# Both Softplus halves of a state-space block in a row on ScalarE at slot 24, with a new table of slots

## The reference

```
z, x, B, C, dt_raw = split(u @ in_proj_w.T)
dt = softplus(dt_raw @ dt_proj_w.T + dt_proj_b)          # 256 channels per token
h  = exp(dt[..., None] * A) * h + (dt * x)[..., None] * B # a scan over the tokens, 32 states per channel
y  = sum over states of h * C;  y = (y + x * D) * silu(z) @ out_proj_w.T
mlp = silu(xn @ gate_w.T) * (xn @ up_w.T) @ down_w.T      # 704 hidden
```

## Time and profile before

| | us |
|---|---|
| median of 3 runs | 1143.21 (1143.1 to 1143.37) |
| the profiled execution | 1142.64 |
| its span | 1140.6 |
| PE, DVE, POOL, ACT busy | 1027.5, 1009.3, 931.2, 627.9 |
| first scan of tiles 0 to 7 starts at | 38.3, 150.3, 280.0, 407.6, 536.1, 663.6, 792.0, 919.5 |

### The profile page before, as it was taken

How to read it: one execution, slowest core, us unless ns; L and a number is a source line. 1 busy time by engine, 2 the same in 40 slices (tenths; PEclk the granted TensorE clock), 3 DMA queues, 4 the chain that set the end, 5 groups by cost and what they waited for, 6 DMA issues and landing times.

```text
span 1140.6 us, 13548 instructions
## 1 busy us (share of the span) xinstructions
PE 1027.5 (90%) x3844; PEld 537.2 (47%) x3844; DVE 1009.3 (88%) x1133; ACT 627.9 (55%) x1235; POOL 931.2 (82%) x540
## 2 busy tenths in 40 slices
PE   3566689999999999999999999999999989899998
PEld 1222134546454554546453554546453543446777
DVE  4689899999999999999999999999999989997342
ACT  4464675548655675548655675548655554443320
POOL 2689899888999899888999899888999989886100
PEclk9696689999999999999999999999999989899999
DMA  6999899998979798998989798988979797860000
GB/s 230 227 209 196 187 237 245 234 194 187 230 180 218 166 232 192 210 198 189 227 186 214 166 239 185 216 196 189 232 176 204 165 229 163 175 148 19 0 1 18
DMA packets 120121, 208.41 MB, mean 183 GB/s; under 512 B 16816, under 2 KB 25968, under 8 KB 119920
## 3 DMA queue, kind: packets, MB, share of 16 engines
q1 hardware_dynamic: 118320, 203.85, 79.8%
q0 software_dynamic: 1008, 3.67, 0.9%
q10 hardware_dynamic: 720, 0.04, 0.0%
HBM read 178.65 MB, written 12.06 MB: 167 GB/s over the span
## 4 chain that ended last, share of the span: by engine, by line
PE 59%; POOL 15%; issue 8%; ACT 8%; DVE 7%; DMA 1%; SPq 1%; DVEq 0%; POOLq 0%; ACTq 0%
PE p_r L560 17%; PE p_r L549 11%; POOL h_s L1352 9%; PE p_y L515 7%; PE p_r L555 6%; PE p_dt L504 5%; DVE h_s L1083 4%; POOL bt_s L1322 3%; PE p_r L566 2%; PE p_dt L660 2%; PE p_r L660 2%; ACT p_dt L716 2%; PE p_r L535 2%; ACT tok L765 2%; PE p_r L670 1%
## 5 line engine op out<-in xcount | busy, mean ns | idle before, releaser
L1352 POOL TENSOR_TENSOR h_s<-h_s,c_s 128x1024 f32<-128x1024 f32 x255 | 601.9, 2365 | 69.9 <-DVE h_s L1083 52.2
L716 ACT ACTIVATE p_dt<-p_dt,an_s 128x512 f32<-128x512 f32 x400 | 260.7, 660 | 274.2 <-PE p_dt L504 273.9
L1083 DVE TENSOR_TENSOR_SCAN h_s<-p_dt,carry,bt_s 128x512 f32<-128x512 f32 x256 | 319.4, 1271 | 7.8 <-ACT p_dt L716 7.2
L1083 DVE TENSOR_TENSOR_SCAN h_s<-p_dt,bt_s 128x512 f32<-128x512 f32 x256 | 303.2, 1211 | 15.5 <-ACT p_dt L716 13.3
L504 PE MATMUL p_dt<-kdt,pick_s 128*128 128x512 f32 x400 | 253.5, 647 | 56.3 <-DVE h_s L1083 44.2
L1322 POOL TENSOR_TENSOR bt_s<-bt_s,b_s 128x1024 f32<-128x1024 f32 x101 | 239.0, 2366 | 12.3 <-DMA bt_s<-dx_rows 7.5
L560 PE MATMUL p_r<-nT,w_s 128*128 128x512 f32 x448 | 208.3, 601 | 0.3
L1066 DVE TENSOR_TENSOR bt_s<-bt_s,p_b 128x1024 f32<-128x1024 f32 x155 | 186.3, 1202 | 8.8 <-DMA bt_s<-dx_rows 8.8
L504 PEld LDWEIGHTS p_dt<-kdt,pick_s 128*128 128x128 f32 x400 | 78.6, 200 | 193.8 <-DVE h_s L1083 104.1
L515 PE MATMUL p_y<-h_s,ysel_s 128*32 128x512 f32 x1024 | 143.1, 633 | 14.8 <-POOL h_s L1352 14.5
L549 PE MATMUL p_r<-nT,gu_s 128*128 128x512 f32 x308 | 144.6, 599 | 5.9 <-ACT nT L916 5.9
(11 more groups left out here) (153 smaller groups left out, 955.4 us busy)
## 6 DMA issues: line engine op xcount, KB each, us to landing
bt_s<-dx_rows SPq DMA_DIRECT2D x512, 256.0 KB, 5.7
dtr_s<-dt_rows SPq DMA_DIRECT2D x224, 128.0 KB, 6.5
kdt<-st_dt SPq DMA_DIRECT2D x64, 128.0 KB, 5.4
tok<-in_x SPq DMA_DIRECT2D x8, 512.0 KB, 8.5
xo<-in_x SPq DMA_DIRECT2D x8, 512.0 KB, 3.8
xr_s<-xb_s SPq DMA_DIRECT2D x64, 64.0 KB, 5.5
b_s<-xb_s SPq DMA_DIRECT2D x64, 64.0 KB, 5.2
dx_rows<-dx_s SPq DMA_DIRECT2D x16, 256.0 KB, 6.5
```

Source lines behind the costliest of these rows:

```text
L716: A(p_dt[DT_BANK[u]][:, :], dt_in, ACT.Exp, scale=an_s[:, c:c + 1]).then_inc(a_dA, 1)
L1083: V.tensor_tensor_scan(h_s[:, u % 8, :], p_dt[DT_BANK[u]][:, :], bt_s[:, u % 16, :], carry[:, u:u + 1] if par else 0.0, ALU.mult, ALU.add) ...
L1352: G.tensor_tensor(h_s[:, two, :], h_s[:, two, :], c_s[:, h, :].unsqueeze(1).broadcast_to([P, 2, T]), ALU.mult)\
```

## The change

The matmul of `dtp1` moves from slot 53 to slot 24, right behind that of `dtp0`. Both Softplus stand in slot 25 one after the other. The second writes to a new SBUF tile `dt1_s`, which takes the place of `dt_s` and of the PSUM bank for that half; its rounded copy, low part and `dt * x` stay in slots 55 and 57. The bank of `dtp1` is free after its Softplus. The table of slots is a new one. POOL gets pair 8 of tile 0 and pairs 20 and 31 of tiles 2, 4 and 6, 7 pairs in all, from DVE.

```
-POOL_FIRST = [0, 3, 6, 9, 13, 16, 19, 22, 26, 29]
+POOL_FIRST = [0, 3, 6, 8, 9, 13, 16, 19, 22, 26, 29]
-POOL_EVEN = [0, 3, 5, 9, 11, 13, 16, 19, 21, 24, 25, 27, 29]
+POOL_EVEN = [0, 3, 5, 9, 11, 13, 16, 19, 20, 21, 24, 25, 27, 29, 31]
 PLAN = [
-    ("out", 1, 4, 5, 6), ("z", 0, 2, 9, 9), ("z", 1, 2, 9, 9), ("dtr", 0, 2, 10, 13), ("hT", 0, 4, 12, 12),
+    ("out", 1, 4, 5, 6), ("z", 0, 2, 9, 9), ("z", 1, 2, 9, 9), ("dtr", 0, 2, 10, 12), ("hT", 0, 4, 11, 11),
...
-    ("up", 3, 2, 19, 22), ("gate", 4, 2, 20, 22), ("up", 4, 2, 23, 23), ("dtp0", 0, 1, 24, 25),
-    ("gate", 5, 2, 24, 24), ("down", 0, 12, 24, 28), ("down", 1, 12, 29, 31), ("c0", 0, 2, 31, 35),
+    ("up", 3, 2, 19, 22), ("gate", 4, 2, 20, 21), ("up", 4, 2, 22, 22), ("gate", 5, 2, 23, 23),
+    ("dtp0", 0, 1, 24, 24), ("dtp1", 0, 1, 24, 24), ("down", 0, 12, 24, 28), ("down", 1, 12, 29, 31),
+    ("c0", 0, 2, 31, 33), ("xT", 0, 4, 35, 35), ("xT", 1, 4, 35, 35), ("w1", 0, 2, 37, 37), ("w3", 0, 2, 37, 38),
...
+DT1_SLOT = 53
-W2_SLOT = 15
+W2_SLOT = 14
+        dt1_s = sb("dt1_s", [P, T])
...
             def keep_rows(t, par, h):
-                    sp.wait_ge(a_dt, t * 2 + h + 1)
-                    sp.dma_start(dt_rows[par, h], dt_s[:, :]).then_inc(l_dt_rows, 16)
+                    sp.wait_ge(a_sp if h else a_dt, t * 2 + 2 if h else t + 1)
+                    sp.dma_start(dt_rows[par, h], (dt1_s if h else dt_s)[:, :]).then_inc(l_dt_rows, 16)
...
-            freed = {"uT": (a_uT, 2), "dtr": (a_dtr, 1), "xb": (a_xb, 1), "dtp0": (v_dtl, 2), "dtp1": (v_dtl, 2),
+            freed = {"uT": (a_uT, 2), "dtr": (a_dtr, 1), "xb": (a_xb, 1), "dtp0": (v_dtl, 2), "dtp1": (a_sp, 2),
...
             def softplus(t, h):
-                A(v, v, ACT.Softplus, bias=par_s[:, 4 + h:5 + h]).then_inc(a_sp, 1)
+                if h and t:
+                    act.wait_ge(g_dx, t * 2)
+                    act.wait_ge(v_dtl, t * 2)
+                    act.wait_ge(a_dth, t * 2)
+                    if t >= 2:
+                        act.wait_ge(l_dt_rows, (t - 1) * 32)
+                A(dt1_s[:, :] if h else v, v, ACT.Softplus, bias=par_s[:, 4 + h:5 + h]).then_inc(a_sp, 1)
...
-                            if u == ENDS[f"dtp{h}", 0] + 1:
+                            if u == ENDS["dtp1", 0] + 1 + (3 if i == -1 and h else 0):
                                 softplus(nt, h)
-                            if u == ENDS[f"dtp{h}", 0] + 2 and not (known(i) and i == -1 and h):
+                            if u == (DT1_SLOT if h else ENDS["dtp1", 0]) + 2 and not (i == -1 and h):
                                 keep_dt(nt, h)
...
-                            if u == ENDS[f"dtp{h}", 0] + 4 and not (known(i) and i == -1 and h):
+                            if u == (DT1_SLOT if h else ENDS["dtp1", 0]) + 4 and not (i == -1 and h):
                                 drive_rows(nt, other, h)
```

More of the change, by code:

```diff
@@ L772, in softplus @@
                 act.wait_ge(mm["dtp"], t * 2 + h + 1)
-                A(v, v, ACT.Softplus, bias=par_s[:, 4 + h:5 + h]).then_inc(a_sp, 1)
+                if h and t:
[5 more added lines that the diff above has]
+                A(dt1_s[:, :] if h else v, v, ACT.Softplus, bias=par_s[:, 4 + h:5 + h]).then_inc(a_sp, 1)
             def keep_dt(t, h):
                 m = t * 2 + h
-                v = ring[BANK[f"dtp{h}", 0]][:, :]
                 act.wait_ge(a_sp, m + 1)
-                if h or from_tile(t, 1):
-                    act.wait_ge(g_dx, m)
-                    if m > 2:
+                if h:
+                    v = dt1_s[:, :]
+                else:
+                    v = ring[BANK["dtp0", 0]][:, :]
+                    if t:
+                        act.wait_ge(g_dx, m - 1)
+                    if t >= 2:
                         act.wait_ge(l_dt_rows, (m - 2) * 16)
-                A(dt_s[:, :], v, ACT.Copy).then_inc(a_dt, 1)
+                    A(dt_s[:, :], v, ACT.Copy).then_inc(a_dt, 1)
                 if h:
@@ L1106, in low_dt @@
                 dve.wait_ge(a_dth, m + 1)
-                V.tensor_tensor(st_dt[:, 1, :], ring[BANK[f"dtp{h}", 0]][:, :], st_dt[:, 0, :].bitcast(F32),
+                V.tensor_tensor(st_dt[:, 1, :], dt1_s[:, :] if h else ring[BANK["dtp0", 0]][:, :], st_dt[:, 0, :].bitcast(F32),
                                 ALU.subtract).then_inc(v_dtl, 1)
@@ L1308, in drive_rows @@
                 m = t * 2 + h
-                pool.wait_ge(a_dt, m + 1)
+                pool.wait_ge(a_sp if h else a_dt, t * 2 + 2 if h else t + 1)
                 pool.wait_ge(l_xrep[h], (t + 1) * 64)
@@ L1312, in drive_rows @@
                     pool.wait_ge(l_rows, m * 16)
-                G.tensor_tensor(dx_s[:, :], dt_s[:, :], xr_s[:, par, h, :], ALU.mult).then_inc(g_dx, 1)
+                G.tensor_tensor(dx_s[:, :], (dt1_s if h else dt_s)[:, :], xr_s[:, par, h, :], ALU.mult).then_inc(g_dx, 1)
             def drive(i, k):
```

## The result

The changed kernel takes 1155.93 us (median of 4 runs, 1155.35 to 1157.37), the kernel before beside it 1143.15 (1142.69 to 1143.37): a ratio of 1.0118, 95% interval 1.0103 to 1.0132, so 12.8 us slower. The forecast was 1140.9, range 1132.5 to 1147.0. It was wrong in its sign, and the time lies outside its range.

A forecast was written before the change was run, and what follows sets the result against it. PE, DVE and POOL share the bound, by stretch of a tile. Terms of -1.8 (tile 0), -4.4, +3.0, +3.0, -4.2 and +2.1 sum to -2.3 us, forecasting 1140.9 us, range 1132.5 to 1147.0.

The forecast's parts named there:

- leg B: Stretch of a tile from down to slot 57, taken as set by PE and DVE together.
- given back: In odd tiles, down to slot 57 gets 1.0 us shorter for PE without dtp1, offsetting its cost: 0 net.
- The loads: Fourteen table loads of slot 54 go: 4.4 us gained at odd tile ends, 1.3 in tile 0.
- dtp1 in leg A: From gate to down, set by PE, the moved matmul adds 1.0 us in each of tiles 1 to 6.
- The gate order: Ahead of the gate stage, one exp fewer before PE's awaited copy: 0.6 us in tiles 1 to 7, -4.2 us.
- c0: Ahead of w1, its earlier copy delays the variance of slot 33 by 0.7 us: +2.1 us over even tiles.
- POOL's pairs: Two more pairs in even tiles make POOL 1.0 us later at the seam: 3 x 1.0 = +3.0 us.
- The signs: Expected trace marks: 17 table loads, DVE waits gone, POOL later, odd tiles about 2 us shorter, even about 2 longer.
- Rival 2: DVE sets down to slot 57, so odd tiles regain nothing, and gate order gives nothing: +4.9, 1148.1 us; chance 0.17.
- Rival 3: Longer ACT block in slot 25 reaches DVE and PE in tiles 1 to 6: +4.0 us, 1144.9; chance 0.08.
- Rival 1: Even tiles pay nothing, as PE has 1.0 us spare from gate to down: -10.4, 1132.8 us; chance 0.32.

The follow-up runs named there:

- pairs_before: Changed kernel with the three lists of POOL's pairs set back to those of the kernel before; 1155.98 us, ratio 1.0123.
- both_before: Changed kernel with the w1, w3 and w2 rows and POOL's pair lists both set back to those of before; 1144.13 us, ratio 1.0021.
- w_after: Kernel before with the change's rows for w1, w3 and w2, dtp1 still in slot 53; 1153.67 us, ratio 1.0112.
- late rows: `both_before` with the change's rows from slot 49 on (w1 parts 6 and 7, w2 part 1); 1148.66 us, ratio 1.0063.
- early ones: `both_before` with the change's rows of slots 39 to 44 (w1 parts 2 to 4, w3 part 1); 1148.91 us, ratio 1.0079.
- no_loads: Kernel before with the Softplus of slot 54 of tiles 1 to 7 replaced by a Square that needs no table; 1137.58 us, ratio 0.9963.
- dtp_twice: Kernel before with the matmul of dtp0 made twice in a row in slot 24; 1144.77 us, ratio 1.0032.
- pairs_after: Kernel before with the change's three lists of POOL's pairs; 1142.60 us, ratio 1.0004.
- w_before: Changed kernel with the w1, w3 and w2 rows set back to those of before; 1148.42 us, ratio 1.0063.
- gate_uT: `gate_early` with two more of the change's rows, c1 in slots 0 to 1 and uT in slot 2; 1135.18 us, ratio 0.9934.
- gate_early: Kernel before with only hT part 0, dtr and gate part 0 placed earlier as in the change; 1138.15 us, ratio 0.9965.

## Why the prediction was wrong

**The step that failed.** The sum has no term for the rows of w1, w3 and w2. The working took leg B from "PE ends what follows", read off 53.7 busy of 53.8 us, so that its length would be PE's work whatever the order, and from there "In odd tiles leg B is 1.0 us shorter for PE, and I take it as given back: 0". Its part from w1 to w2's end measured 55.0 us in odd tiles where the working implies 52.8. Moving seven pairs of matmuls by up to four slots, one of them past another, and w2's second part by one slot, costs 11.9 us in all (`pairs_before` less `both_before`), and in the kernel before a ratio of 1.0112 (`w_after`). A stretch in which PE has no gap isn't one in which PE's order is free: the spreads lie between the stages' matmuls, and each carries an exp, a scan and the bank for the next spread. What came in its place are waits of PE for DVE: 0.94 us in slot 55 by the late rows, and 1.1 us in an odd tile by the early ones, in three short waits of which most hides in PE's busy rows.

**The terms.** Other terms with a kernel of their own were nearer.
- The loads, 4.4 + 1.3 us forecast: 4.2 by `no_loads`, made of 0.8 after odd tiles, 0.2 after even ones and 1.2 in tile 0. The forecast adds 1.47 for them and 1.0 for dtp1 in an odd tile. Together they gave 1.0 in `both_before`. With the change's rows they gave 0.8 (w1 to the next gate in `pairs_before` and `w_after`, 79.2 and 80.6 us, 0.6 of it the gate order's). So the two overlap, and no run tells how much of it is whose.
- dtp1 in leg A, 1.0 a tile: 0.6. Given back from w1 to w2's end: 0.9, if the rows of before stand there; nothing with those of the change.
- The gate order, 4.2: 4.0 by its ratio, 0.3 x 7 = 2.1 by the cuts.
- c0, 2.1: the power of slot 32 does come 0.65 us later after down's end, as forecast, but down's end to w1 is 8.0 against 7.9, so 0.1 a tile.
- POOL's pairs, 1.0 at each of three seams: 0.8 in `pairs_after`, 1.5 in the changed kernel, 2.6 in `w_before`, by what else holds the seam. The row was as forecast, POOL's instruction of slot 57 comes 1.1 us later after the power than the earlier trace rows had it (652.11 is the pair before it):

```profile
608.06 1.02 POOL L1390 TENSOR_TENSOR rs<-ve,half_s 128x4 f32<-128x4 f32 x1 [1.16 <-ACT nm L916]
...
652.11 0.19 POOL L1357 TENSOR_TENSOR carry<-h_s,one_s 128x2 f32<-128x2 f32 x1 [0.32 <-DVE h_s L1094]
...
657.01 0.66 POOL L1357 TENSOR_TENSOR carry<-h_s,one_s 128x2 f32<-128x2 f32 x1
```

**The signs.** Those named for each step were nearly all there: 17 loads, no wait where the earlier trace rows had them, 1.3 us in slot 27, the late POOL (with one wait left, of 0.32 us). The one that counted said otherwise: odd tiles 3.0 us longer and not 2 shorter, even ones 1.3 longer.

**The rivals.** Rival 2 had the sign and one true result, that odd tiles don't get dtp1's microsecond back; its reason, DVE full for 46.65 of 47.0 us, is wrong, since `both_before` leaves DVE as full and gets 0.9 us. Its 1148.1 lacks the table too, and it gives nothing for the gate order, which gave 0.3 us a tile. Rival 3 is 0.1 to 0.25 us a tile and not 0.66. Rival 1 is refuted by `dtp_twice`. The 1.1 us that it took to be spare in PE's leg A was misread: 559.30:603.30 ends 3.1 us behind down (600.18), and its idle time is the wait for the spread after c0. Up to down's end PE is busy for 40.8 of 40.9 us.

What stays open: 0.3 us a tile ahead of down, how the gain of the loads and that of dtp1 share the seam, and what of `gate_uT`'s 3 us over `gate_early` is its two rows' and what the clock's.

## What to carry to other kernels

When a change comes with a new table of slots, price its rows one by one, above all in stretches where an engine is full without a gap: that row says who is behind, not that the order there is free. Test the table in the old kernel first; here one run of it would have shown 12 of the 13 us. And a wait that goes is worth what the next wait behind it lets through: the loads were worth 0.8 us after an odd tile by themselves, and they and dtp1's microsecond together no more than 1.0. An engine that is busy in every row can be waiting all the same, where its records overlap: compare the times from start to start with those of a run that is faster.
